# A graph network's dense stages: the nodes dealt into chunks of 512, 512 and 226 instead of 512, 384 and 354

## What is computed

```python
# layer 0 (a = edge_attr_64 [E, 64])
msg = relu(x[src] + a @ W_e + b_e)
h = (1 + eps) * x + segment_sum(msg, dst)          # [1250, 512]
h = silu(batchnorm(h @ W1 + b1, g1, beta1))        # 512 -> 1024, statistics over the nodes
y = silu(batchnorm(h @ W2 + b2, g2, beta2))        # 1024 -> 512
x = layernorm(x + y)
# layer 1 (c = edge_attr_128 [E, 128])
m = relu(concat(x[src], c) @ V1.T + b1) @ V2.T + b2
agg = segment_sum(m, dst)
r, z, n = GRU gates of (agg @ W_ih.T + b_ih) and (x @ W_hh.T + b_hh)   # 3 x 512 each
h_new = (1 - z) * n + z * x
x = layernorm(x + x + gamma * (h_new - run_mean) * rsqrt(run_var + 1e-5) + beta)
```

## Time and profile before

| | us |
|---|---|
| median of 3 runs | 839.12 |
| the three runs | 836.28, 839.12, 842.10 |
| profiled execution, from its first to its last instruction | 836.84 |
| PE busy in it | 781.1 (93%) |
| DVE busy | 636.8 (76%) |
| ACT busy | 449.6 (54%) |
| POOL busy | 362.0 (43%) |
| mean granted clock of TensorE | 0.981 of full |

### The profile page before, as it was taken

One profiled execution on the slowest core, in us unless ns is written; L12 is line 12 of the kernel. 1 busy time (PEld: TensorE's weight loads), 2 busy tenths in 40 slices (PEclk: granted clock), 3 DMA queues, 4 the chain that ended last, 5 costly groups with the idle time before them and its releaser, 6 DMA issues.

```text
span 836.8 us, 11419 instructions
## 1 busy us (share of the span) xinstructions
PE 781.1 (93%) x3734; PEld 628.3 (75%) x3734; DVE 636.8 (76%) x1126; ACT 449.6 (54%) x809; POOL 362.0 (43%) x381
## 2 busy tenths in 40 slices
PE   7898999888999999798699999999999999999995
PEld 5565666555689999686477777788777798989895
DVE  7788899989989816387699999999984372626255
ACT  4887899888854413211467777778762121111122
POOL 6777777777500000023777777777720000000011
PEclk9999999999999999899799999999999999999998
DMA  8999988888620050014688888888830210200011
GB/s 229 314 304 303 275 259 264 255 249 252 181 98 1 8 195 0 1 51 159 203 261 295 252 259 256 260 255 256 255 115 4 76 76 1 76 1 1 1 51 72
DMA packets 49389, 134.38 MB, mean 161 GB/s; under 512 B 8265, under 2 KB 8521, under 8 KB 48944
## 3 DMA queue, kind: packets, MB, share of 16 engines
q0 software_dynamic: 26720, 87.58, 35.1%
q1 hardware_dynamic: 22116, 45.59, 16.7%
q10 hardware_dynamic: 492, 0.45, 0.2%
HBM read 128.47 MB, written 5.12 MB: 160 GB/s over the span
## 4 chain that ended last, share of the span: by engine, by line
PE 61%; DMA 11%; POOL 10%; DVE 8%; issue 6%; ACT 3%; SPq 0%; DVEq 0%; POOLq 0%; ACTq 0%
PE banks L518 39%; PE banks L545 11%; POOL raw L448 9%; DMA raw<-in_x,src_sb 6%; PE banks L575 4%; PE banks L576 3%; DVE msg_lo L1114 3%; DMA raw<-table_dram,src_sb 2%; DVE raw L1122 2%; DMA x_in<-in_x 2%; PE banks L573 1%; PE banks L598 1%; ACT banks L853 1%; PE banks L589 1%; DVE stats L1251 1%
## 5 line engine op out<-in xcount | busy, mean ns | idle before, releaser
L448 POOL DMA_INDIRECT raw<-in_x,src_sb x167 | 169.7, 1016 | 52.5 <-issue 44.5
L448 POOL DMA_INDIRECT raw<-table_dram,src_sb x167 | 164.2, 983 | 59.8 <-issue 38.4
L470 POOL TENSOR_TENSOR moments<-moments,minus_half 128x1 f32<-128x1 f32 x32 | 20.3, 635 | 302.3 <-DVE moments L1257 302.3
L853 ACT ACTIVATE banks<-raw 128x512 f32<-128x512 f32 x166 | 99.1, 598 | 79.7 <-DMA raw<-table_dram,src_sb 52.6
L1122 DVE TENSOR_TENSOR raw<-banks,raw 128x512 f32<-128x512 f32 x168 | 114.4, 681 | 20.3 <-PE banks L545 15.8
L1114 DVE SCALAR_TENSOR_TENSOR msg_lo<-raw,msg_hi 128x512 fp32r<-128x512 f32 x168 | 114.1, 679 | 4.5 <-ACT msg_hi L897 3.8
L575 PE MATMUL banks<-msg_hi,hot 128*128 128x512 f32 x293 | 115.9, 396 | 0.7 <-DVE agg L1137 0.4
L576 PE MATMUL banks<-msg_lo,hot 128*128 128x512 f32 x293 | 114.9, 392 | 0.0
L897 ACT ACTIVATE msg_hi<-raw 128x512 fp32r<-128x512 f32 x168 | 104.3, 621 | 14.4 <-DVE raw L1122 13.9
L545 PE MATMUL banks<-We_hi,attr 97*128 97x512 f32 x167 | 87.7, 525 | 16.5 <-ACT banks L853 15.1
L1114 DVE SCALAR_TENSOR_TENSOR msg_lo<-banks,msg_hi 128x512 fp32r<-128x512 f32 x125 | 84.8, 678 | 2.1 <-ACT msg_hi L897 1.8
(11 more groups left out here) (170 smaller groups left out, 1725.1 us busy)
## 6 DMA issues: line engine op xcount, KB each, us to landing
attr_sb<-in_attr SPq DMA_DIRECT2D x84, 128.0 KB, 4.6
attr_sb<-in_attr SPq DMA_DIRECT2D x42, 256.0 KB, 3.8
Wg_raw<-in_Wg SPq DMA_DIRECT2D x3, 1536.0 KB, 6.3
raw<-in_x,src_sb POOLq DMA_INDIRECT x167, 4.8
raw<-table_dram,src_sb POOLq DMA_INDIRECT x167, 4.1
x_in<-in_x SPq DMA_DIRECT2D x5, 512.0 KB, 14.3
rows<-in_x SPq DMA_DIRECT2D x1, 2560.0 KB, 12.2
table_dram<-table_sb SPq DMA_DIRECT2D x9, 256.0 KB, 2.0
```

Source lines behind the costliest of these rows:

```text
L448: pool.indirect_dma_start(rows_of(L, t), None, tables[L], bass.IndirectOffsetOnAxis(ap=src_sb[:, t:t + 1], axis=0)).then_inc(gathered[t % ...
L470: nc.gpsimd.tensor_tensor(moments[:, slot * 4 + 2:slot * 4 + 3], moments[:, slot * 4 + 1:slot * 4 + 2], minus_half[:, 0:1], ALU.pow).then_ ...
L853: return nc.scalar.activation(to, of, ACT.Copy)
```

## The change

The table of chunks becomes (0, 512), (512, 512), (1024, 226). Chunk 1 then holds the blocks 4 to 7 and not 4 to 6, and chunk 2 the blocks 8 and 9 and not 7 to 9. The low parts of the messages `m_lo` are one tile per chunk, so the third is placed 2 KB further on.

```diff
-NODE_CHUNKS = [(0, 4 * P), (4 * P, 3 * P), (7 * P, N - 7 * P)]
+NODE_CHUNKS = [(0, 4 * P), (4 * P, 4 * P), (8 * P, N - 8 * P)]
...
         m_lo = [at(f"m_lo{q}", [P, KD, w], F32R, offset)
-                for q, ((_, w), offset) in enumerate(zip(NODE_CHUNKS, (B0 + 32 * KB, A0 + 52 * KB, A0 + 58 * KB)))]
+                for q, ((_, w), offset) in enumerate(zip(NODE_CHUNKS, (B0 + 32 * KB, A0 + 52 * KB, A0 + 60 * KB)))]
```

## The result

| | before | after |
|---|---|---|
| median of 11 runs, us | 839.62 | 845.43 |
| lowest, us | 836.28 | 840.03 |
| ratio of the undisturbed runs, 95% interval | | 1.0045 [1.0028, 1.0063] |
| profiled execution: its span, us | 836.84 | 842.30 |
| its own time, us | not recorded | 843.92 |

The changed kernel is slower by 0.45% (0.28 to 0.63), 3.8 us (2.4 to 5.3). The forecast was +2.4 us; both lie within 1%. The ratio is taken over the undisturbed runs, whose means are 844.3 and 840.6 us; one execution of the kernel before, of 882.57 us, is not among them. The medians lie further apart, 5.8 us: the new one, 845.43, is 3.9 us over the forecast of 841.5, inside the full range of 836.5 to 847 and just outside the 838 to 845 that the terms alone gave.

A forecast was written before the change was run, and what follows sets the result against it. PE's matmuls were taken to bound the dense stages, DVE's and ACT's operations the end; +1.5 + 2.2 + 1.3 - 1.1 - 1.3 - 0.2 = +2.4 us gave 841.5 us, range 836.5 to 847 with the runs' spread.

The forecast's parts named there:

- Step 1: Sets of three matmul widths in W1, W2, V2 and the first three m of the gates: 38 x 0.04 = +1.5 us.
- Step 2: Last m up to the second turning: wider group 10 costs +4.1, the 36 group 11 matmuls save 1.9; +2.2 us.
- Steps 3 and 4: DVE at the second turning, four blocks instead of three, +1.3 us; last group's DVE operations and tanh, 226 columns, -1.1 us.
- Step 5: Last turning has two blocks instead of three: -1.3 us.
- Step 6: End of W2: eviction and statistics of the last chunk, 128 columns fewer: -0.2 us.
- The cover at the second turning: PE reaches the second turning 0.8 us after group 10's last DVE operation, so the turning does not wait for DVE.
- The rival of 100 ns: Narrow 226-column matmul not held by the weight load, 100 ns each: -2.4 us in all, 836.7 us; 6%.
- 124 ns: Rival: weight load and overhead add up for the 226-column matmul: +9.4 us in all, 848.5 us; 6%.
- the unsplit rate: Rival: 226-column matmuls fall to the rate of unsplit float32, 0.37 us each: +138 us, 980 us; 7%.
- the full record: Rival: the load's full record, 0.19 us, becomes the distance between narrow matmuls: +42 us, 883 us; 1%.

The follow-up runs named there:

- the last-m run: Chunks 512, 512, 226 in the last m of the gates alone, against the kernel before; one execution: +2.12 us to the first turning, +1.4 us in all.
- the ladder: Kernel before with matmuls of 512 down to 64 columns added behind its last block on PE; one execution: 111.6 ns between starts at 192 columns, 231.0 at 512.

## Why the prediction was right, and by how much it was off

The mechanism was right and the sum was short by 1.1 us of 3.5. By its steps:

- **Step 1, the sets of three: +1.5 forecast, +2.6 measured.** This is the term that was mis-sized. W1 and W2 gave 1.25; V2 and the gates up to the first turning 0.88 + 2.58 = 3.46, of which the wide half of group 10 is 2.1 (the last-m run: 2.12), so 1.35 for 22 sets. That is 0.07 a set instead of 0.04. Two small things make it: the narrow matmul took 111 to 112 ns and not 110, since the floor of an fp32r matmul is 111.6 and not the 109 that the transposes show, whose operands are float32; and 512 columns are 233 ns over the whole of W1 and W2, where the twelve I read gave 232.
- **Step 2, the last m: +2.2 forecast**, 2.12 + 0.17 = 2.3 measured.
- **Steps 3 and 4: +0.2 forecast, +0.25.** Four blocks took 5.55 us, the last group 834.89 - 830.92 = 3.97.
- **Step 5: -1.3 forecast, -1.37**, and -1.36 at the lower clock. The prediction had no term for that clock: it moves the end by 0.46 us, in either kernel.
- **Step 6: -0.2 forecast, -0.29.**
- **The cover at the second turning: 0.8 us forecast, 0.8 measured.** In all five profiles with the wide group 10 the second turning came 14.1 us after the first.

The prediction's own working has two small slips. The rival of 100 ns adds up to -2.5 us and not -2.4; and the distances lie 13 to 17 ns over N/2.4 + 2.5, not 14 to 17. Neither touches the forecast.

The rival of 100 ns is out by the ladder, as are 124 ns, the unsplit rate and the full record. The Trainium skill, "TensorE: Matmul & The Clock Gate", sections "Back-to-back issue gap" and "LDWEIGHTS (loading the stationary operand)", gave an estimate of +5.5 us, from a gap of N/2.4 + 2.5 ns and a load of 107 ns for 128 columns. Here the load's floor is 111.6 ns, the distance 12 to 18 ns over the columns from 256 up, and the loss of 3.5 us lies between that estimate and mine. By these figures the load would bound 226 columns, and the ladder shows that it does.

What stays open: the interval of the measured difference (2.4 to 5.3 us) holds 3.5 and 2.4 alike, so that it is 3.5 rests on the stretches. That the floor costs 226 columns 6 ns is shown. Why the distance grows by 0.439 ns a column, where one column per cycle of 2.4 GHz is 0.417, and why 512 columns take 2 ns more in W1 and W2 than on the ladder, is not.

## What to carry to other kernels

When a product is split along the moving axis, the sum of the columns is what counts until one piece falls under the load of the next weights; here that is some 240 columns of fp32r against 128 weight columns. Above it, three splits of W1 and W2 into the same number of matmuls cost the same to within 0.4%. A split also sets what lies ahead of the last dependent step: here a wider second-to-last chunk delayed it by all its extra columns, and of what the last group saved on PE half lay behind that step, hidden behind the vector work. And where edges or clock spread by 3 us, cut the profile into stretches between fixed instructions: those that PE filled without a pause repeated to 0.05 us, on different chips too. Compare a stretch behind a pause only with one at the same granted clock.

## What the runs showed of the hardware

- The floor for a matmul with 128 fp32r weight columns is 111.6 ns from start to start, from 226 down to 64 columns; with 96 weight columns it was 85.0, with 64 61.9 and with 32 60.0 (each at 128 moving columns). The transposes, with float32 operands, stood at 109. At a granted clock of 0.50 they stood at 213. Loads of 128, 96 and 64 weight columns had records of 190, 164 and 136 ns.
- Above the floor an fp32r matmul cost 6.4 ns and 0.439 ns a column, to 0.5 ns, from 226 to 512 columns.
- In the pause behind W2 and the short pieces of work in it the granted clock averaged 0.60 to 0.64. It was back at 1.00 some 0.6 us behind the first table matmul in the kernel before and 3.5 us behind it in the first profile of the changed one, 0.8 in the second. The table matmuls took from 35.7 to 39.0 us, by this and by a second stretch at the lower level near their end in some.
- Ahead of the third turning PE was idle for 2.5 to 4.3 us. Over its first four transposes the granted clock was 0.88 to 1.00 in some executions and 0.50 in others, with old and new chunks alike, and the last stretch took 0.46 us more in the latter.
- On two chips the edges, with their gathers, took 100 to 115 us longer in all than on the others (the same bytes, 141 to 143 GB/s over the span instead of 160 and 161), while the dense stretches agreed to 0.1 us.
